# A gated cross-attention block: the last batch in a new order on every engine, the low parts of four weight pieces on GpSimd, statistics and gated sums in another order

## The reference, cut to what matters

```python
# B = 8 batches, 224 tokens (latents), 750 context rows, width 512, 8 heads of 64
x = x + tanh(g_xattn) * xattn(ctx, layernorm(x))
x = x + tanh(g_ffn) * ffn(layernorm(x))

xattn:  xn = layernorm(ctx, gm, bm); ln = layernorm(latents, gl, bl)
        q = ln @ Wq;  k, v = split(concat([xn, ln]) @ Wkv)      # 974 keys
        out = softmax(q k^T * 8) v per head;  return out @ Wout
ffn:    h = square(relu(x @ W_fc^T))                            # 2048 neurons
        y = h @ W_proj^T
        five steps of a leaky neuron with threshold 1 driven by y; return spikes / 5
```

## Time and profile before

| | |
|---|---|
| median of 3 runs | 1059.72 us |
| profiled execution, its own time | 1059.53 us |
| span of its trace | 1057.7 us |
| PE busy | 1030.8 us, 97% |
| DVE busy | 803.0 us, 76% |
| ACT busy | 594.7 us, 56% |
| POOL busy | 312.5 us, 30% |
| TensorE clock granted | full speed in all 40 slices |

### The profile page before, as it was taken

The page is one execution under the profiler, slowest core; times in us unless marked ns, Lnnn a source line. Parts: engine busy times, 40 slices in busy tenths (PEclk is TensorE's granted clock), DMA queues, the critical chain, the costliest instruction groups (busy, mean ns, idle before and its releaser), DMA issues.

```text
span 1057.7 us, 18993 instructions
## 1 busy us (share of the span) xinstructions
PE 1030.8 (97%) x6913; PEld 838.0 (79%) x6913; DVE 803.0 (76%) x1231; ACT 594.7 (56%) x1147; POOL 312.5 (30%) x285
## 2 busy tenths in 40 slices
PE   5999999999999999999999999998999999999997
PEld 5778778877877877887887787776788888998886
DVE  7488888978988888897898898879534565585766
ACT  5558547655654844764665584466456433455535
POOL 4343534335434363334533435334000000000000
PEclk9999999999999999999999999999999999999999
DMA  6402010101201201010020200121430000200011
GB/s 196 133 1 65 14 35 19 57 3 32 75 0 35 75 0 35 31 45 9 25 75 0 74 0 0 35 91 47 143 129 29 1 1 20 100 2 36 25 60 41
DMA packets 31891, 47.43 MB, mean 45 GB/s; under 512 B 2284, under 2 KB 11516, under 8 KB 31852
## 3 DMA queue, kind: packets, MB, share of 16 engines
q1 hardware_dynamic: 31716, 46.74, 13.7%
q10 hardware_dynamic: 136, 0.17, 0.1%
HBM read 39.56 MB, written 7.34 MB: 44 GB/s over the span
## 4 chain that ended last, share of the span: by engine, by line
PE 91%; DVE 7%; DMA 1%; issue 1%; ACT 1%; SPq 0%; DVEq 0%; ACTq 0%
PE work L483 40%; PE score L649 13%; PE work L636 13%; PE heads_out L588 9%; PE score L562 8%; PE score L498 2%; PE heads_out L600 1%; PE score L836 1%; DMA xin<-in_ctx 1%; DVE top L1328 1%; DVE probs L1364 1%; DVE mx L1336 0%; PE maxes L575 0%; DVE bn L1426 0%; DVE on L1411 0%
## 5 line engine op out<-in xcount | busy, mean ns | idle before, releaser
L1832 POOL TENSOR_TENSOR dsum<-dsum,probs 125x448 f32<-125x448 f32 x186 | 225.9, 1215 | 14.6
L483 PE MATMUL work<-wv,xT 128*125 128x512 f32 (+1 forms) x768 | 188.2, 399 | 0.9 <-DVE kst L1376 0.8
L483 PE MATMUL work<-xT,wk 128*128 128x486 f32 (+2 forms) x768 | 184.1, 390 | 0.5 <-DVE kst L1376 0.5
L483 PEld LDWEIGHTS work<-wv,xT 128*125 128x125 f32 (+1 forms) x768 | 137.8, 183 | 40.7 <-issue 4.6
L636 PE MATMUL work<-zT,wf 128*128 128x512 f32 (+1 forms) x768 | 164.3, 364 | 1.3 <-DVE wf L1492 1.3
L483 PEld LDWEIGHTS work<-xT,wk 128*128 128x128 f32 x768 | 140.1, 188 | 30.1 <-issue 4.6
L636 PEld LDWEIGHTS work<-zT,wf 128*128 128x128 f32 x768 | 131.5, 189 | 24.3 <-issue 2.0
L956 ACT ACTIVATE probs<-score 125x448 f32<-125x448 f32 (+1 forms) x256 | 119.9, 548 | 53.3 <-PE score L562 53.2
L1829 POOL TENSOR_TENSOR dsum<-probs 125x448 f32<-125x448 f32 x31 | 35.7, 1150 | 371.2 <-ACT probs L962 371.2
L1364 DVE TENSOR_TENSOR probs<-probs,mx 125x1792 f32<-125x1792 f32 x64 | 130.2, 2044 | 1.1
L649 PE MATMUL score<-hT,wp 128*128 128x512 f32 (+1 forms) x576 | 117.5, 354 | 0.0
(11 more groups left out here) (195 smaller groups left out, 1436.4 us busy)
## 6 DMA issues: line engine op xcount, KB each, us to landing
xin<-in_ctx SPq DMA_DIRECT2D x42, 250.0 KB
neuron<-in_L_ffn_W_fc SPq DMA_DIRECT2D x16, 256.0 KB, 3.0
neuron<-in_L_ffn_W_proj SPq DMA_DIRECT2D x16, 256.0 KB, 2.8
xres<-in_x SPq DMA_DIRECT2D x16, 224.0 KB, 2.5
x_scratch<-xres SPq DMA_DIRECT2D x16, 224.0 KB, 2.3
xin<-in_x SPq DMA_DIRECT2D x14, 224.0 KB, 9.9
zt<-x_scratch SPq DMA_DIRECT2D x3, 1024.0 KB, 5.7
fin<-x_scratch SPq DMA_DIRECT2D x3, 1024.0 KB, 5.6
```

The lines of the kernel that those rows point to most:

```text
L483: mm = pe.matmul(bank, lhs(i, k), rhs(j, k), start=(n == 0), stop=(n == len(passes) * chunks - 1))
L1832: pool.tensor_tensor(total[0:ROWS[t]], total[0:ROWS[t]], tile(t), ALU.add).then_inc(dchain if t < TILES - 1 else dsum_done, 1)
```

## The change

No arithmetic changes. Work moves between places in the lists of the engines, and between two engines:

- A new semaphore `fw_lo_early` stands for pieces 0 to 3. Their low parts are made by POOL, between `denominators(7, 1)` and `denominators(7, 2)`, no longer by DVE. Whoever waited for the low part of a piece asks `lo_ready`.
- The loop, PE: `max_transposes(b, 1)` stands ahead of `keys_queries(b, 2, (2,))`. DVE: `query_maxima(b, 1)` stands between the two `statistics`; the last two `folds` of pair 1 stand ahead of the first `gated_residual`.
- The last batch: PE begins with `values(7, 4)`; `attend(7, 2)` and `attend(7, 3)` move ahead, among the `up` products. ACT: `heads_hi(7, 1)` moves ahead of `split_weights(4)`, `heads_hi(7, 2)` ahead of `relus(0, 4)` and `split_weights(6)`. DVE: `normalise(7, 1)` moves ahead of the last folds of pair 3, `split_weights(4)` and `heads_lo(7, 1)` around `subtract(7, 6)`, `split_weights(5)` ahead of `last_sums`.
- The prelude: `maxima(0, 0)` stands behind `kq_lo_parts(0, 2, 0)`, and `row_columns` turns the value row into `heads_out` instead of `maxes`, so that it can't meet the squares of the maxima.

The summary that came with the change also names rows of maxima that are left in SBUF. The diff has no such edit.

```diff
+        EARLY = 4
+        def lo_ready(n):
+            return (fw_lo_early, n + 1) if n < EARLY else (fw_lo, n + 1 - EARLY)
...
@@ SP, PE (up, down), ACT (take_y): every wait on fw_lo
-                    sp.wait_ge(fw_lo, n - SLOTS + 1)
+                    sp.wait_ge(*lo_ready(n - SLOTS))
...
@@ PE batch
                 values(b, 5)
+                max_transposes(b, 1)
                 keys_queries(b, 2, (2,))
-                max_transposes(b, 1)
@@ PE last_batch
+                values(b, 4)
                 max_transposes(b, 1)
-                values(b, 4)
+                values(b, 5)
                 max_rows(b, 1)
-                values(b, 5)
                 keys_queries(b, 2, (2,))
...
                 max_transposes(b, 3)
                 up(0, 2, 1, 2)
                 max_rows(b, 3)
+                attend(b, 2)
                 up(0, 2, 2, 3)
                 up(0, 3)
+                attend(b, 3, maxes)
+                totals(b, 2)
                 up(0, 4)
-                attend(b, 2)
-                totals(b, 2)
-                attend(b, 3, maxes)
                 totals(b, 3, maxes)
                 up(0, 5)
@@ PE row_columns, and ACT where it reads the row
-                    mm = pe.transpose(maxes[:, c * P:(c + 1) * P], vrow[:, c * P:(c + 1) * P], ident[:, :])
+                    mm = pe.transpose(heads_out[:, c * P:(c + 1) * P], vrow[:, c * P:(c + 1) * P], ident[:, :])
@@ ACT last_batch
                 exponentials(b, 5)
+                heads_hi(b, 1)
                 split_weights(4)
                 relus(0, 1)
                 squares(0, 0)
+                exponentials(b, 6)
                 relus(0, 2)
-                exponentials(b, 6)
                 exponentials(b, 7)
                 squares(0, 1)
                 relus(0, 3)
-                heads_hi(b, 1)
                 split_weights(5)
                 squares(0, 2)
+                heads_hi(b, 2)
                 relus(0, 4)
                 act.wait_ge(pv_done, NA * PAIRS)
                 split_weights(6)
-                heads_hi(b, 2)
                 heads_hi(b, 3)
@@ DVE last_batch
                 group_lo(0, 0, 1, 2, 3)
-                split_weights(0)
                 subtract(b, 4)
                 subtract(b, 5)
                 folds(b, 3, 1)
-                split_weights(1, 2)
+                normalise(b, 1)
                 folds(b, 3, 2, 3)
                 maxima(b, 3)
-                split_weights(3)
                 query_maxima(b, 3)
+                split_weights(4)
                 subtract(b, 6)
-                split_weights(4)
+                heads_lo(b, 1)
                 subtract(b, 7)
-                normalise(b, 1)
                 h_lo_part(0, 0)
+                split_weights(5)
                 last_sums(b)
                 h_lo_part(0, 1)
-                split_weights(5)
-                heads_lo(b, 1)
                 normalise(b, 2)
@@ DVE batch
                 statistics(b + 1, 0)
+                query_maxima(b, 1)
                 statistics(b + 1, 1)
-                query_maxima(b, 1)
...
-                folds(b + 1, 1, 2)
+                folds(b + 1, 1, 2, 3)
                 gated_residual(b, 0)
-                folds(b + 1, 1, 3)
                 maxima(b + 1, 1)
@@ DVE prelude
+            kq_lo_parts(0, 2, 0, first=True)
             maxima(0, 0)
-            kq_lo_parts(0, 2, 0, first=True)
@@ POOL batch
-                for p in range(1, PAIRS - 1 if last else PAIRS):
-                    denominators(b, p)
+                denominators(b, 1)
+                if last:
+                    for n in range(EARLY):
+                        pool.wait_ge(fw_hi, n + 1)
+                        pool.tensor_tensor(piece(n, 1), stage(n), piece(n, 0).bitcast(F32),
+                                           ALU.subtract).then_inc(fw_lo_early, 1)
+                denominators(b, 2)
+                if not last:
+                    denominators(b, 3)
```

More of the change, by code:

```diff
@@ L290, in flamingo_block @@
         fw_lo = sem("fw_lo")
+        fw_lo_early = sem("fw_lo_early")
         zt_in = sem("zt_in")
@@ L631, in up @@
                     pe.wait_ge(relu_done, g * FC + (j - 1))
-                pe.wait_ge(fw_lo, PIECES.index(("up", j)) + 1)
+                pe.wait_ge(*lo_ready(PIECES.index(("up", j))))
                 for m in range(lo, hi):
@@ L645, in down @@
                     pe.wait_ge(y_done, g * DC)
-                pe.wait_ge(fw_lo, PIECES.index(("down", j)) + 1)
+                pe.wait_ge(*lo_ready(PIECES.index(("down", j))))
                 for d in ds:
@@ L1248, in _ @@
             act.wait_ge(v_shift_mm, 1)
-            act.activation(shift[:, 2, :, 0:1], maxes[:, :].rearrange("p (c r) -> p c r", c=DC)[:, :, LT:LT + 1],
+            act.activation(shift[:, 2, :, 0:1], heads_out[:, :].rearrange("p (c r) -> p c r", c=DC)[:, :, LT:LT + 1],
                            ACT.Copy).then_inc(v_shift, 1)
@@ L1266, in take_y @@
                     act.wait_ge(spk_done, g * 2)
-                act.wait_ge(fw_lo, len(PIECES))
+                act.wait_ge(*lo_ready(len(PIECES) - 1))
                 for d in range(DC):
```

## The result

| | before | after |
|---|---|---|
| median | 1059.99 us, 14 runs (1059.23 to 1062.82) | 1056.92 us, 14 runs (1055.85 to 1059.06) |
| profiled execution | 1059.53 us | 1057.90 us |
| span of its trace | 1057.7 us | 1056.0 us |

The ratio is 0.9968, with a 95% interval of 0.996 to 0.9976: the change makes the kernel 3.1 us faster (0.32%). The forecast was 1058.9 us and no difference that can be told.

What follows compares the result with a forecast made beforehand. PE, busy 97% at full clock, bounds the kernel; a new order can win only about 8 us of idle time. -0.85 + 0 - 0.7 + 0.8 = -0.75 from 1059.53, plus 0.19, gave 1058.9 us; range 1056.6 to 1061.2.

Steps and rivals of the forecast that it cites:

- Prelude: Start of the kernel: PE's wait at `values(0, 0)` for the keys' low part goes, -0.85 us.
- First pass: First pass of the loop: PE's 1.02 us wait moves from `max_rows` to `values(7)`, worth 0.
- Loop: Six later pass boundaries: earlier folds save 0.14 us each, -0.84; taken as -0.7, ends -0.9 and 0.
- the tie: Loop: DVE needs 4.17 us to the queries' low part, PE asks after 4.22; 0.1 late per pass loses the gain.
- Last batch, until the last maxima: Start of the last batch: PE-paced work comes 2.2 us earlier, `rmax` of pair 3 1.7 earlier, at 718.7.
- the 2.01 wait: Start of the last batch: PE waited 2.01 us for `rmax`; it would do `values(7, 4)` first instead.
- To the last exponential: Last batch: DVE's instructions held 0.5 or 0.95 us each by POOL; last exponential ends at 729.8, against 731.46 before.
- E: End of the last batch's last exponential: 731.46 before, forecast 729.8, 727.0 if POOL holds nothing.
- From E to the out projection: End of the last batch: out projection starts at E + 16.1, before E + 13.6; at 745.9, +0.8 us.
- Rival A: Last batch: POOL hardly holds DVE, E near 727.0, last batch wins 2.0, 1056.0 us; chance 0.2.
- Rival B: Last batch: POOL holds all, ACT waits carry on, +2.4, loop tie lost; +1.6 in all, 1061.1 us; chance 0.15.
- the two waits for ACT: Last batch behind E: DVE waits about 2 us ahead of `split_weights(5)` and 1 to 1.5 ahead of `split_weights(6)`.

Runs made afterwards that it cites:

- e11: The changed kernel with DVE's low part of the queries of pair 2 put ahead of the second statistics in the loop; 1056.51 us, ratio 0.9961.
- e3: The kernel before with only the folds moved ahead of the first gated sum; 1056.06 us, ratio 0.9957.
- e2: The kernel before with the loop's three edits alone (max_transposes and query_maxima earlier, folds ahead of the first gated sum); 1056.71 us, ratio 0.9964.
- e6: The kernel before with POOL's additions for pair 2 of the last batch left out but for one short one; last batch 72.28 us instead of 75.54.
- e12: The changed kernel with the queries' low part ahead of the second statistics and the last batch reworked on PE, ACT and DVE; 1053.58 us, ratio 0.9937.
- e8: The changed kernel with the low parts of pieces 0 to 3 back on DVE in their old places; 1059.82 us, ratio 0.9994.
- e9: Prelude and loop as in the changed kernel, last batch's lists and POOL as in the kernel before; 1056.12 us, ratio 0.9958.
- e15: The same kernel as e9, run again on one chip with the changed kernel; 1055.09 us, ratio 0.995.

## Why the prediction was wrong

The mechanism was right in the main and the size was not. The step that failed is a term of the last batch: `last_sums` was put at 4.86 us with what follows, a length read from before, in which POOL held the first sum; after shows 3.92, and that alone is 0.95 of the 1.95 us that the forecast is off. The other 1.0 is three smaller terms: 0.5 in how long POOL holds DVE ahead of the last exponential, 0.3 in the loop and 0.2 in the prelude.

- **Prelude.** Right. The wait at `values(0, 0)` is gone, the trace of after has `values` at 46.89 with no idle time. Prelude and first pass gave 1.05 for 0.85 forecast; from the row product to `values(0, 0)` it is 3.74 before and 2.73 after.
- **First pass.** Right: `e11` and after show the wait at `values(7)` for the queries, 1.23 us for 1.02 before at another instruction. It can be had with another edit (0.7, `e11`).
- **Loop.** Right in kind; a pass lasts 87.18 (forecast 87.2), -1.0 in all for -0.7. `e3` against `e2` shows that the folds bring all of it; with the two other edits a pass is 0.04 longer (87.18 for 87.14), so the tie broke by next to nothing.
- **Last batch, until the last maxima.** The sum was right (`rmax` of pair 3 comes 1.6 earlier for 1.7), the reasoning was not complete. I put the end of the 2.01 wait down to PE's new list. The folds alone end it (`e3`), and so the two are worth 2.18 together, not one each. Because I costed the folds only at the six boundaries (0.14 each) and not at the seventh, which is `rmax` of the last batch, I did not see that the largest gain of the change was there, nor that it left next to nothing (0.2 us) for the new lists to gain before the last exponential.
- **To the last exponential.** Close. ACT's last exponential of after ends at 727.22 + 0.56 = 727.78. The last batch starts 1.50 us earlier than in before, so in the time of before E is 729.28; 729.8 was forecast. Held were a subtraction by 0.28, `heads_lo` by 0.89, the next by 0.96; the split ahead of them was free. The forecast had 0.5 and 0.95 twice, and half of a split, 2.85 in all for 2.13 measured. It was 0.5 us too late.
- **From E to the out projection.** Mis-sized: 15.13 us (727.78 to 742.91), forecast 16.1. The idle times were right (2.56 for 2, 1.55 for 1 to 1.5). The term that was wrong is `last_sums`: its 4.86 us were taken from before, where POOL held the first of the sums by 0.94; `e6` has it at 1.08, after at 1.09, and the whole takes 3.92 in after (730.66 to 734.58). The next sum, of the same size, was in the trace of before at 1.09.
- **Rival A** read the same 2.03 as "as short as alone" and so as evidence that POOL holds little. It was evidence of the contrary. A did not happen: DVE was held as the forecast has it. What came out is near A's time for other reasons.
- **The sum.** The forecast's own terms give 1058.97 (1059.53 - 0.75 + 0.19), which it put as 1058.9. Against the lengths, 0.2 more in the prelude, 0.3 in the loop, 0.5 for E and 0.95 for the sums make 1.95, the whole difference between -0.75 and -2.70. The rest to the -3.07 of the medians is left to the scatter and, perhaps, to the clock.
- **Rival B** (slower) had its mechanism right in part: the two waits for ACT exist and cost 1.3 us against the old lists. They did not turn the sign, because the folds paid for them.

## What to carry to other kernels

When several edits aim at one wait, cost each alone and then all together: here two of them took 2.0 and 2.2 us off one engine's list, and 2.2 as a pair, and what one of them cost behind that made it a loss. Take the length of an instruction from its shortest twin of the same shape, and ask who runs beside it before calling a row undisturbed. And an idle time ahead of an engine may be the time in which its neighbour on the same memory finishes, so removing it gives back less than its length.

## What the runs showed of the hardware

- DVE's instructions with two operands in SBUF took 0.3 to 1.0 us longer beside POOL's additions of 1.15 us (the subtraction 2.30, 2.54 and 2.98 for 2.02, a split 1.62 and 1.67 for 0.68). POOL's additions then took 1.9 to 2.1 each on average (11.23 us for six in before, 12.45 in `e12`), the longest recorded 2.8. The same instruction may be free of it: the first sum took 1.09, 1.64, 1.66 and 2.03 us in four orders.
- TensorE's clock went to half for 3.4 us (6.8 in `e8`) in some executions, after waits of 2.0 to 2.5 us in the last batch, and there in no trace whose longest wait is 1.8 us or less. A wait of 2.0 to 2.2 did not always do it: before and `e6` with 2.0, after and `e11` with 2.19 have full clock there.
- In the prelude four of 17 traces have half clock at about 20 us, behind waits of 1.5 to 1.8 us. It costs 1.6 us there: from the end of this wait to the product for the queries `e9` needs 11.70 us (18.85 to 30.55) and before 10.09 (18.79 to 28.88). These four have their row product at 45.2 to 45.4, the others at 42.5 to 44.2, so the start scatters by another 1.6 without it. It is a large part of the scatter of this kernel.
- A length inside the trace repeats to 0.1 us, where no half clock falls on a stretch that PE bounds (697.40 and 697.38 for `e9` and `e15`, 698.75 twice for after), and medians of 5 runs of the same kernel do not repeat to 1 (1056.12 and 1055.09).
